# A four-part decoder block on one Trainium2 core: score banks, load order, and where the shared expert's first block is prepared

## The reference, cut to what matters

```python
x = x + tanh(g_xattn[0]) * L0_xattn(layernorm(x), ctx, pos, pos, Wq, Wkv, Wout, bout)   # 32 heads of 8, axial rope
x = x + tanh(g_ffn[0])   * L0_ffn(layernorm(x), ...)     # top 2 of 8 experts, and a shared expert with a sigmoid gate
x = x + tanh(g_xattn[1]) * L1_xattn(layernorm(x), ctx, mask, Wq, Wk, Wv, Wo)
x = x + tanh(g_ffn[1])   * L1_ffn(layernorm(x), ...)
```

## Time and profile before

| | us |
|---|---|
| median of 3 runs | 1870.15 (1867.95 to 1874.39) |
| the profiled execution, its own time | 1873.31 |
| its span, first to last instruction | 1871.3 |
| PE busy | 1632.6 (87%) |
| DVE busy | 1164.6 (62%) |
| ACT busy | 726.3 (39%) |
| POOL busy | 412.1 (22%) |

### The profile page before, as it was taken

One profiled execution on the slowest core, in us unless ns is written; L12 is line 12 of the kernel. 1 busy time (PEld: TensorE's weight loads), 2 busy tenths in 40 slices (PEclk: granted clock), 3 DMA queues, 4 the chain that ended last, 5 costly groups with the idle time before them and its releaser, 6 DMA issues.

```text
span 1871.3 us, 42250 instructions
## 1 busy us (share of the span) xinstructions
PE 1632.6 (87%) x14740; PEld 1369.2 (73%) x14740; DVE 1164.6 (62%) x3002; ACT 726.3 (39%) x1478; POOL 412.1 (22%) x448
## 2 busy tenths in 40 slices
PE   0788888886899889999789999999999998699998
PEld 0555555553677668999678888888888887487887
DVE  3477777776656756555566666666666665365654
ACT  1355555553222222555333333433333333234443
POOL 0555555550312421000121112221112110000000
PEclk9899999997999999999889999999999998799999
DMA  7556556561100101544300000000000000000000
GB/s 193 123 111 116 109 105 116 111 113 31 42 28 29 40 23 43 165 140 126 138 21 21 25 20 25 22 25 20 25 20 24 24 14 6 5 12 22 11 23 23
DMA packets 127211, 107.12 MB, mean 57 GB/s; under 512 B 10426, under 2 KB 120307, under 8 KB 126620
## 3 DMA queue, kind: packets, MB, share of 16 engines
q1 hardware_dynamic: 120924, 89.13, 20.4%
q0 software_dynamic: 6208, 16.95, 2.8%
HBM read 49.29 MB, written 56.77 MB: 57 GB/s over the span
## 4 chain that ended last, share of the span: by engine, by line
PE 56%; DVE 24%; issue 9%; ACT 3%; DMA 3%; SPq 2%; DVEq 2%; POOL 1%; ACTq 0%; another core or an unknown queue 0%; POOLq 0%; PEldq 0%
PE bank L513 11%; PE bank L515 10%; PE bank L514 10%; PE bank L985 3%; PE bank L585 3%; PE bank L576 3%; PE bank L1013 2%; PE bank L599 2%; PE bank L540 2%; DVE probs_b L2208 2%; DVE rm_b L2205 2%; PE bank L614 2%; DVE probs_a L1666 1%; DVE x L2109 1%; DVE oT_b_lo L2197 1%
## 5 line engine op out<-in xcount | busy, mean ns | idle before, releaser
L1533 POOL TENSOR_TENSOR probs_b<-probs_b,rs_b 128x512 f32<-128x512 f32 x64 | 66.8, 1043 | 483.7 <-DVE rs_b L2218 483.4
L513 PE MATMUL bank<-xT_b_hi,m_hi 128*128 128x256 f32 x512 | 153.8, 300 | 20.1 <-ACT qT L1343 11.9
L1364 ACT ACTIVATE probs_b<-probs_b 128x512 f32<-128x512 f32 x64 | 40.4, 632 | 324.1 <-DVE probs_b L2208 324.1
L513 PE MATMUL bank<-n_hi,oT_b_hi 128*128 128x256 f32 x512 | 150.0, 293 | 5.7 <-DVE x L2176 5.7
L514 PE MATMUL bank<-xT_b_hi,m_lo 128*128 128x256 f32 x512 | 145.7, 285 | 0.0
L515 PE MATMUL bank<-xT_b_lo,m_hi 128*128 128x256 f32 x512 | 145.5, 284 | 0.0
L514 PE MATMUL bank<-n_hi,oT_b_lo 128*128 128x256 f32 x512 | 145.4, 284 | 0.0
L515 PE MATMUL bank<-n_lo,oT_b_hi 128*128 128x256 f32 x512 | 145.3, 284 | 0.0
L1141 ACT ACTIVATE probs_a<-probs_a 128x512 f32<-128x512 f32 x128 | 80.1, 626 | 134.1 <-DVE probs_a L1666 133.1
L985 PEld LDWEIGHTS bank<-ctxT_b,qT 128*128 128x128 f32 x1024 | 126.7, 195 | 2.8
L985 PE MATMUL bank<-ctxT_b,qT 128*128 128x64 f32 x1024 | 123.2, 274 | 0.0
(11 more groups left out here) (315 smaller groups left out, 4818.8 us busy)
## 6 DMA issues: line engine op xcount, KB each, us to landing
sorted_x<-zeros SPq DMA_DIRECT2D x16, 2112.0 KB, 14.7
xg<-sorted_x SPq DMA_DIRECT2D x71, 128.0 KB, 2.1
sorted_y<-ys SPq DMA_DIRECT2D x71, 128.0 KB, 1.9
w_raw<-in_w SPq DMA_DIRECT2D x16, 408.0 KB, 3.8
x<-in_x SPq DMA_DIRECT2D x4, 1024.0 KB, 7.7
cx_raw<-in_ctx SPq DMA_DIRECT2D x32, 128.0 KB
out<-x SPq DMA_DIRECT2D x8, 512.0 KB, 2.9
ctxT_a<-in_ctxT SPq DMA_DIRECT2D x16, 128.0 KB, 2.1
```

The costliest lines, as they stand in the source:

```text
L513: pe.matmul(dst, lh, rh, start=start, stop=False, skip_group_check=True)
L1533: pool.tensor_tensor(probs_b[b], probs_b[b], rs_b[:, b, :].unsqueeze(2).broadcast_to([P, G1, S]), ALU.mult).then_inc(s["b_probs"], 1)
```

## The change

- **Score banks.** `scores0` writes in turn banks 0, 1, 3 and 6, and waits only for the pair before the last one. To free them, the transposed probabilities have bank 2 alone (`turn_probs` of n waits for `pT_copy` of n-1), and the values go through bank 7; ACT copies that bank at once into a new tile `v_raw` (`v_keep`, one more 128 x 512 copy a round, ahead of exp(6)), and `v_copy` reads from there. PE does the values at t = 5 instead of 6.
- **Loads.** One constant less is loaded. ctxT_a of round 0, wk and wq go ahead of x. The table loads are cut in two: the first 512 columns (rounds 0 to 3) ahead of wv and wo, the other 1536 behind them and behind the router's weights, which are loaded here instead of after the attention. PE starts keys, transposition and queries of round 0 once wk and wq are in. DVE and POOL wait for the rest of the tables before their first round. SP's loop loads ctx for round i+1 behind values(i).
- **The shared expert's first block.** In the last round DVE takes the statistics of eight tiles behind pair 0, normalises block 0 behind pair 1, and makes the two low parts behind pair 3 and behind the first residual; PE transposes block 0 into bank 7 at t = 5 and 9, ACT copies it at t = 6 and 10. The router's weights are split before round 0. Logits come before block 0; the rest of the prologue (back_g, largest_g, counts_g, weights_g, place_g, slots_g) goes between the steps of block 0.

```diff
+        def score_bank(n):
+            return bank[(0, 1, 3, 6)[n % 4]]
...
+            load_context(0)
+            for dst, src in ((wk0, "wk0"), (wq0.rearrange("p k n -> p (k n)"), "wq0")):
+                sp.dma_start(dst, a[src]).then_inc(s["wqk_loaded"], 16)
             load_x(0)
...
+            sp.wait_ge(s["tables_stored"], 32)
+            EARLY = 4 * P
+            load_tables(slice(0, EARLY), "tables_loaded")
...
+            sp.dma_start(rw0_raw.rearrange("p k m -> p (k m)"), a["rw0"]).then_inc(s["sel0_loaded"], 16)
+            load_tables(slice(EARLY, NT * S), "tables_rest")
...
+            with sp.Fori(0, NA - 1) as i:
+                sp.wait_ge(s["a_v_psum"], START + 1 + i)
+                load_context(i + 1)
+                load_round(i)
+            load_round(NA - 1)
...
             def values(i):
-                pe.wait_ge(s["a_v_ready"], START + i * 8)
-                vb = bank[6][:, :].rearrange("p (b n) -> p b n", b=4)
+                pe.wait_ge(s["a_q_read"], START + i + 1)
+                vb = bank[7][:, :].rearrange("p (b n) -> p b n", b=4)
...
-                pe.wait_ge(s["a_centred"], START + i * NS + 2 * p)
+                pe.wait_ge(s["a_centred"], START + i * NS + 2 * p - 2)
...
             def turn_probs(i, n):
                 pe.wait_ge(s["a_exp"], START + i * NS + n + 1)
-                pe.wait_ge(s["a_pT_ready"], START + i * NS + n - 1)
+                pe.wait_ge(s["a_pT_ready"], START + i * NS + n)
...
-                        if t == 6:
+                        if t == 5:
                             values(i + 1)
...
+                    elif t in (5, 9):
+                        turn_g(0, (t - 5) // 4)
...
+            def v_keep(i, first=False):
+                act.wait_ge(s["a_v_psum"], START + i + 1)
+                if not first:
+                    act.wait_ge(s["a_v_ready"], START + i * 8)
+                act.activation(v_raw.rearrange("p b n -> p (b n)"), bank[7][:, :], ACT.Copy).then_inc(s["a_v_raw"], 1)
...
             def attend0(i, first=False, last=False):
                 for t in range(NS + 5 if last else NS):
+                    if t == 6 and not last:
+                        v_keep(i + 1)
+                    if last and t in (6, 10):
...
+                        xh_g(0, (t - 6) // 4)
...
-                    if p == 2 and last:
-                        stats_g(0)
+                    if p == 0 and last:
+                        stats_g(0, 2 * FT)
+                    if p == 1 and last:
...
+                        norm_g(0)
+                    if p == 3 and last:
+                        xl_g(0, 0)
                 if last:
                     weigh0(i, 2)
                     resid0(i, 0)
+                    xl_g(0, 1)
                     weigh0(i, 3)
                     resid0(i, 1)
...
             logits_g(0)
-            back_g(0)
-            place_g(0)
...
                     if t < NS0:
                         gate_up_g(i, t)
+                    if i == 0 and t == 0:
+                        back_g(0)
+                    if i == 0 and t == 3:
+                        place_g(0)
```

More of the change, by code:

```diff
@@ L190, in build @@
         maskrow = w1.take("maskrow", S)
+        validb = w1.take("validb", B)
         assert w1.at <= w0.at
@@ L647, in _ @@
             queries(0, 1)
+            pe.wait_ge(s["w0x_loaded"], 208)
             values(0)
@@ L1163, in _ @@
             xT_copy(0)
+            v_keep(0, first=True)
             rounds(act, NA, attend0)
@@ L1272, in _ @@
                         silu_g(i, t)
+                    if i == 0 and t == 1:
+                        halves_g(0)
                     if t >= 1:
@@ L1682, in resid0, with norm_g, xl_g @@
                                         op0=ALU.mult, op1=ALU.add).then_inc(s["a_resid"], 1)
+            def norm_g(i):
+                if i >= 2:
+                    ve.wait_ge(s["g_xT_psum"], (i - 1) * KT)
+                    ve.wait_ge(s[f"rows_moved{i % 2}"], 16 * TOP * FT * (i // 2))
+                for t in range(FT):
+                    st.done(normalise(f0["xn"][i % 2][:, t:t + 1, :], i * FT + t))
+                st.wait()
+                ve.sem_inc(s["g_xn_ready"], 1)
+            def xl_g(i, k):
+                ve.wait_ge(s["g_xh_ready"], i * KT + k + 1)
+                ve.tensor_tensor(f0["xl"][i % 2][:, k, :], turned(i)[:, :], f0["xh"][i % 2][:, k, :], ALU.subtract).then_inc(
+                    s["g_xl_ready"], 1)
             def attend0(i, first=False, last=False):
@@ L1712, in _ @@
             queries(0)
+            ve.wait_ge(s["sel0_loaded"], 16)
+            st.done(ve.tensor_copy(rw0_hi, rw0_raw))
+            st.wait()
+            st.done(ve.tensor_tensor(rw0_lo, rw0_raw, rw0_hi, ALU.subtract))
+            st.wait()
+            ve.sem_inc(s["rw_split"], 1)
+            ve.wait_ge(s["tables_rest"], 64)
             attend0(0, first=True)
@@ L1896, in tiles_of @@
                 return slice(i * FT, (i + 1) * FT)
-            def norm_g(i):
-                if i >= 2:
-                    ve.wait_ge(s["g_xT_psum"], (i - 1) * KT)
-                    ve.wait_ge(s[f"rows_moved{i % 2}"], 16 * TOP * FT * (i // 2))
-                for t in range(FT):
-                    st.done(normalise(f0["xn"][i % 2][:, t:t + 1, :], i * FT + t))
-                st.wait()
-                ve.sem_inc(s["g_xn_ready"], 1)
-            def xl_g(i, k):
-                ve.wait_ge(s["g_xh_ready"], i * KT + k + 1)
-                ve.tensor_tensor(f0["xl"][i % 2][:, k, :], bank[6][:, :], f0["xh"][i % 2][:, k, :], ALU.subtract).then_inc(
-                    s["g_xl_ready"], 1)
             def largest_g(i):
@@ L2052, in _ @@
                         product_g(i, t)
+                    if i == 0 and t == 0:
+                        largest_g(0)
                     if 1 <= t <= NS0:
                         low_g(i, t - 1)
+                    if i == 0 and t == 2:
+                        counts_g(0)
+                        weights_g(0)
+                    if i == 0 and t == 4:
+                        slots_g(0)
                     if i + 1 < NF:
```

136 lines of the change are left out of this document (62 added, 74 removed).

## The result

The changed kernel takes 1850.22 us (1847.94 to 1853.58, 4 runs), the kernel before, beside it, 1871.88 (1867.95 to 1874.39): a ratio of 0.9886, with an interval from 0.987 to 0.9902. The prediction was 1840, within 1818 to 1856. The profiled execution has a span of 1847.3 us against 1871.3.

What follows compares the result with a forecast made beforehand. Load order and issue time bound the start, nearly PE the rounds, engines waiting in turn the hand-over. -17.5 - 1.5 - 12.5 = -31.5, rounded to -30, took the profiled 1873.31 to 1843.3, median 1840 us; range 1818 to 1856.

Steps and rivals of the forecast that it cites:

- 1. Loads: Start: reordered loads bring the first row maximum from 65.8 to 48 us, gated by the tables' rest; -17.5 us.
- the bound of -24: Start: the larger saving in us, if the rest of the tables is not what ends last.
- 2. Rounds: Attention loop: four score banks, one transposed bank; +0.15 us a round, fewer low-clock spells; -1.5 us, from -7 to +6.
- these spells: Attention loop: low-clock spells follow PE's large gap; shrinking it to 1.7 us removes half of them, -3.5 us.
- 3 and 4. Last round and hand-over: Attention's end 3.5 us later, hand-over to the shared expert's first block 16 us shorter; -12.5 us, from -8 to -16.
- Rival A: Attention loop: PE runs ahead and bounds it, a round 21.2 us against 23.9; -38, total 1804 us; chance 0.12.
- Rival C: Attention loop: single transposed bank makes PE wait for ACT behind every pair, +4.6 us a round; total 1904 us; chance 0.04.
- D: Start: the loads do not start the work sooner, only the other parts gain; -14, total 1856 us; chance 0.06.
- B: Only the edges or less: start -13, last round and hand-over -6, loop +3; -16, total 1854 us; chance 0.15.

Runs made afterwards that it cites:

- Experiment 4: Changed kernel with the rest of the tables issued behind the second context load, DVE and POOL waiting for it only after the first round: 1828.58 us.
- experiment 10: Changed kernel with the tables' rest behind the second context load and ACT's turned-tile copies ahead of the exponentials in even steps: 1826.38 us.
- experiment 3: Changed kernel with ACT's copy of a turned tile ahead of the exponential in even steps: 1832.4 us.
- experiment 6: Changed kernel with scores on two banks in turn again, the single transposed bank and saved copy of the values kept: 1841.08 us.
- experiment 5: The changed kernel timed again in a later job, not a line different: 1837.64 us, ratio 0.982.

## Why the prediction was right, and where not

**1. Loads, -17.5.** Measured -18.3 and -18.4. Rope at 27.4 (27.5), tables issued from 31.1 (31.5), maximum at 47.5 (48), held by the tables' rest. Experiment 4 shows what that gate cost: 8 us by the second round, where the bound of -24 allowed 6.5 more. In experiment 10 it was 5.3 by then, as the first round was a long one again.

**2. Rounds.** +0.17 a round was worked out as +0.15, and the wait of 1.7 us ahead of `turn_probs(3)` was 1.77, with ACT's copy behind exp(4) as its cause: experiment 3 takes it away by moving that copy. The mechanism is right, but that the net agrees is luck. The gain of the four banks is 0.36 (said: 0.1 after the saved copy's 0.4, so 0.5), and the price of the saved copy and the single bank 0.38 (said: 0.4 and 0.25): 0.02 in all. The other 0.14 comes from what the sum did not have, of which 0.09 is the second wait in `largest0`. ACT's pieces cost 35 ns more, inside the 0 to 0.05 us. By the Trainium skill (VectorE: DVE Perf Modes, TRN2 errata) it would be 43 ns, as an estimate from its cycle counts; the measured number is a little less.

The loop came out at +1.8 and +1.2, not -1.5, and the step of the sum that failed is a term that it put at nothing: what the late tables do to the first two rounds behind the first maximum. From the first maximum on they take 48.3 and 47.8 us, against 45.7 before, so +2.6 and +2.1. This is the round behind the tables' wait (26.3 and 25.6 us from key shuffle to key shuffle, where experiment 4, without the wait, has 23.8; its first two rounds take 45.8). The other 13 intervals give -0.9 in both executions: about +2 from their length, and -2.9 from the long rounds, which went from five to three.

The -2.9 is near the -3.5 that was put down for these spells, yet the reason given, that the low clock follows PE's large gap, is refuted by experiment 6: the gap of 2.25 us was there in all of its last twelve full rounds, and the clock in none of them fell. That size was hit by luck.

**3 and 4. Last round and hand-over, -12.5.** The last round cost 0.95 and 1.67 (said 3.5): the sum had taken the middle between the high and the low clock, and PE's work behind its wait was at the low one for a few us only (420.3 to about 423.5 in the first execution). To block 0's sum the hand-over saved 10.0 in the first execution, which has half of the pause in it, and 15.4 in the second (said 16, 14 to 17.7). Together parts 3 and 4 are -9.1 and -13.8, against -12.5. The steps again: turning 9.5 behind against 2.8 inside, routing 3.1.

**Sum.** -31.5 was worked out and -30 put down. The changed kernel run again has a span 35.9 below that of the profiled kernel before and a median 32.7 lower than its neighbour's; the stretches that were touched give -30.9 of it, and blocks 1 to 7 (-3.3) and the rest (-1.7), which were not, the remainder. The first job's 21.7 is smaller by about the 10 us of the pause, of which 5.4 lie ahead of block 0's sum and 4.9 in block 1. Nothing like it was among the rivals. It is about as large as the 10 us by which the median landed above the forecast; that the time stayed inside the range with it was not foreseen.

Rival A (PE-bound) failed on its own condition: PE's wait moved to ACT, and once ACT was mended, to DVE. Rival C's waits came once at 1.77 and once at 0.30 a round and not four times. D was refuted at the start. B's 1854 lies close to the first time, but its start (-13) did not occur, and its -6 for last round and hand-over is approached only with the pause in it (-9.1); in the loop its +3 was no further from the measured +1.8 than the forecast's -1.5.

## What to carry to other kernels

When a buffer takes a wait away, follow the engine that waited to its next semaphore: here it went from the centring to ACT's copy (1.77) to DVE's product (1.74), and 2.23 us of idle time were worth 0.36. More buffers and a new order on the in-order engine between were worth something only together: the new banks alone cost 0.02 a round, the new order alone gave 0.00, both gave 0.25. The added second wait was free where DVE came to it busy and cost 0.09 us where it stood behind the wait that ends last. Split a load by when each part is read, and put the wait there too: the second half of that step gave the 6 us that the first had left, and some of the round behind it. And before a pause in a trace is explained, run the same kernel once more in another job; two experiments here "confirmed" a cause that the third, the fourth and the fifth took away. It also pays to ask of a long wait in a list what the same wait is in a run without trouble: of 50.3 us only some 10 were lost.

## What the runs showed of the hardware

The same program stood at 1850.22 us in one job and at 1837.64 in another, 0.7% apart, while the times of each job agreed within 0.35%. The interval of one job does not cover this. In the slower one PE's semaphore updates came up to 11.8 us behind PE's recorded matmul ends (489.24 against 477.42), where experiment 5 has 0.02 at most, and PE's own wait behind that was 11.93 instead of 1.82.

GpSimd issued a scatter every 1.27 us, back to back (466.24 to 486.7 for 16 of them).

In the changed kernel PE's granted clock fell to the low level in three of the rounds behind the second, with PE's longest wait at 1.77 us (0.93 as the mean of a 25 us window); with two score banks in none from the third on, with 2.25; with part 2 undone in three again, with 2.24. What sets it off was not found.
